# Attention outputs turned by DMA instead of TensorE transposes, the causal mask in one pass, and a new order in the group

## The reference

```python
xn = layernorm(x)                              # x: 8 x 1024 x 256, fp32
Q, K, V = xn @ wq.T, xn @ wk.T, xn @ wv.T      # 16 heads of 16 channels
Q, K = rope(Q), rope(K)
scores = where(causal, Q @ K.T / sqrt(16), -inf)
attn = softmax(scores) @ V                     # 8 x 1024 x 256
s = attn @ wo
g = silu(ffn(xn))                              # hidden 768, integer weights / 127
out = x + s * g
```

## Time and profile before

| | us |
|---|---|
| median of 3 runs | 1221.46 (1220.7 to 1222.96) |
| the profiled execution: its own time | 1220.83 |
| its span in the trace | 1219.1 |
| PE busy | 1176.2 (96%) |
| DVE busy | 971.1 (80%) |
| ACT busy | 880.6 (72%) |
| POOL busy | 638.2 (52%) |

### The profile page before, as it was taken

How to read it: one execution, slowest core, us unless ns; L and a number is a source line. 1 busy time by engine, 2 the same in 40 slices (tenths; PEclk the granted TensorE clock), 3 DMA queues, 4 the chain that set the end, 5 groups by cost and what they waited for, 6 DMA issues and landing times.

```text
span 1219.1 us, 29979 instructions
## 1 busy us (share of the span) xinstructions
PE 1176.2 (96%) x10707; PEld 554.8 (46%) x10707; DVE 971.1 (80%) x1160; ACT 880.6 (72%) x1123; POOL 638.2 (52%) x996
## 2 busy tenths in 40 slices
PE   5999999999999889999999999999999999999997
PEld 3565556656555333334444443444444444444333
DVE  6666666667777689988898899889888988898843
ACT  4554554454444588788888888888888888888884
POOL 5765665765564322444455445554565455445554
PEclk9999999999999899999999999999999999999998
DMA  9755454566642511332323313333144133332122
GB/s 254 191 173 155 141 187 135 157 191 172 167 136 87 147 45 46 98 79 72 97 76 110 97 46 106 73 103 97 49 122 113 45 98 88 97 97 58 59 71 88
DMA packets 157888, 134.81 MB, mean 111 GB/s; under 512 B 49472, under 2 KB 142144, under 8 KB 157760
## 3 DMA queue, kind: packets, MB, share of 16 engines
q1 hardware_dynamic: 157760, 133.08, 38.7%
HBM read 72.61 MB, written 50.33 MB: 101 GB/s over the span
## 4 chain that ended last, share of the span: by engine, by line
PE 61%; ACT 2%; DVE 1%; issue 1%; POOL 1%; ACTq 0%; DVEq 0%; POOLq 0%
PE ps L1380 23%; PE ps L1363 14%; PE ps L794 12%; PE ps L1410 4%; PE ps L802 3%; PE ps L1394 3%; PE ps L1402 2%; ACT pr L1281 1%; DVE mxp L818 1%; PE ps L833 1%; ACT on L1293 0%; POOL ah L1101 0%; POOL zt L1119 0%; DVE yt L1219 0%; ACT ot L1288 0%
## 5 line engine op out<-in xcount | busy, mean ns | idle before, releaser
L818 DVE TENSOR_REDUCE mxp<-ps 128x2 f32<-128x1024 f32 (+2 forms) x576 | 685.3, 1221 | 91.0 <-PE ps L802 50.6
L1281 ACT ACTIVATE pr<-ps 128x1024 f32<-128x1024 f32 x576 | 575.8, 1023 | 100.5 <-PE ps L1363 86.1
L1380 PE MATMUL ps<-pr,vt 128*32 128x512 f32 (+3 forms) x3072 | 315.3, 497 | 0.6 <-POOL pr L1091 0.5
L1363 PE MATMUL ps<-qs,ks 50*128 50x512 f16 (+3 forms) x1536 | 225.6, 329 | 8.6 <-DVE mxp L818 4.2
L794 PE MATMUL ps<-ks,qs 48*128 48x512 f16 (+2 forms) x1792 | 225.2, 304 | 8.2 <-ACT pr L1281 4.8
L1091 POOL TENSOR_SCALAR_AFFINE_SELECT pr<-pr 128x256 f32<-128x256 f32 (+1 forms) x448 | 191.6, 454 | 51.3 <-ACT pr L1281 51.0
L1363 PEld LDWEIGHTS ps<-qs,ks 50*128 50x128 f16 x1536 | 65.4, 93 | 212.7 <-issue 201.6
L674 PE MATMUL ps<-xTh,wguT 128*128 128x512 f16 x384 | 145.8, 380 | 1.2 <-ACT vs L558 1.1
L674 PE MATMUL ps<-xTl,wguT 128*128 128x512 f16 x384 | 145.5, 379 | 0.0
L794 PEld LDWEIGHTS ps<-ks,qs 48*128 48x128 f16 x1792 | 83.0, 94 | 98.6 <-issue 85.0
L849 POOL TENSOR_SCALAR mp<-mneg 32x128 f16<-32x128 f32 x32 | 9.3, 289 | 206.3 <-issue 200.9
(11 more groups left out here) (104 smaller groups left out, 1355.9 us busy)
## 6 DMA issues: line engine op xcount, KB each, us to landing
v_d<-vs SPq DMA_DIRECT2D x16, 1024.0 KB, 5.3
vt<-v_d SPq DMA_DIRECT2D x32, 512.0 KB, 4.0
xs<-in_L_attn_x SPq DMA_DIRECT2D x16, 512.0 KB, 4.5
q_parts_d<-parts SPq DMA_DIRECT2D x16, 512.0 KB, 3.0
k_parts_d<-parts SPq DMA_DIRECT2D x16, 512.0 KB, 3.1
gate_d<-gs SPq DMA_DIRECT2D x16, 512.0 KB, 3.2
qs<-q_parts_d SPq DMA_DIRECT2D x64, 128.0 KB, 3.1
ks<-k_parts_d SPq DMA_DIRECT2D x64, 128.0 KB, 3.1
```

The lines of the kernel that those rows point to most:

```text
L818: dve.tensor_reduce(dst, ps[:, slot:slot + 2, :].rearrange("p t (n s) -> p (t n) s", s=w), axis=AX.X, op=ALU.max).then_inc(keep["max_dve"] ...
L1281: act.activation(probs(step, s).rearrange("p (t j) s -> p t j s", t=2)[:, :, hs[0]:hs[-1] + 1, 0:w], ps[:, slot:slot + 2, 0:w * len(hs)].r ...
L1363: ins = pe.matmul(ps[:, slot + t, o:o + w], ks[g][r, j, kb * P:(kb + 1) * P], qs[g][r, j, lo:lo + w], start=o == 0, stop=True, skip_group_ ...
L1380: ins = pe.matmul(ps[VW * j:VW * (j + 1), O0, lo - c * CH:CH], vt[g % 2][:, kb, j, :], probs(step, s)[:, j, at:at + w], start=first, stop= ...
```

## The change

1. V is written with 16 columns of ones a head, so each sum comes on 16 rows. `take_output` stays; then SP moves each head's 16 rows of values into `oc` and its 16 rows of sums into `sc`, by DMA from `ot` (eight DMAs of 32 KB a half, `move_output`). In `oc` and `sc` the channels are on the partitions, 128 at a time, as the product with wo wants them. L1394, the copies `on`, `an` and `ah`, the transposes L1402 and the copies L1298 go.
2. Per tile: DVE takes the reciprocal of `sc` (128 x 256), POOL multiplies `oc` by it and splits the result into `aT`.
3. The mask: `pick` and `future` hold factors over 64 rows whose products give the mask of a 128 x 128 square, so one pass does. POOL builds them in two lots, in chunks (0, 1) and (5, 0).
4. `transpose_max` uses a transpose instead of a product with the identity.
5. ORDER, V_AT and all places in the group are new. In the last group DVE does the scaling and the additions of seven tiles; at the end the splits are shared by ACT, DVE and POOL.

```diff
-        ORDER = "EMEMEMEMEMEMEEMEMEMMEMEMEMEMEMEMEMEM"
+        ORDER = "EMEMEMEMEMEMEMMEMEMEMEMEMEMEMEMEMEEM"
...
-            V_AT = (9, 12, 16, 23, 27, 30, 35, TURNS + 1, TURNS + 4, TURNS + 6)
+            V_AT = (13, 16, 18, 24, 30, 33, 35, TURNS + 2, TURNS + 5, TURNS + 8)
-            TAKE1, OUT1, NORM1 = 3, 18, 14
-            TAKE0, OUT0, NORM0 = 8, 21, 14
-            MAXT, NEG, SPLIT_AT = 25, 12, 10
-            HALVE, ADD = (0, 7), (8, 17)
-            COPY, SCALE = (11, 9), (17, 12)
-            TR, EV, WO, MUL = (7, 26), (4, 13), (15, 33), (8, 16)
+            TAKE1, TAKE0, MAXT, NEG, SPLIT_AT = 5, 8, 25, 12, 11
+            INVERT, HALVE, ADD = (0, 3), (1, 6), (7, 13)
+            WO, MUL = (11, 21), (7, 10)
...
+                def move_output(step, c):
+                    b, g = step
+                    if g == 0 and b > 1:
+                        sp.wait_ge(t_lo.sem, t_lo.after((b - 2, (c + 1) * CT - 1)))
+                    sp.wait_ge(o_act.sem, o_act.after(step, c + 1))
+                    for j in range(GH):
+                        r, o = g % 2 * GH * DK + j * DK, j * VW
+                        sp.dma_start(oc[b % 2][r:r + DK, g // 2, c * CH:(c + 1) * CH], ot[o:o + DK, c]).then_inc(o_in[b % 2][c], 16)
+                        sp.dma_start(sc[b % 2][r:r + DK, g // 2, c * CH:(c + 1) * CH], ot[o + DK:o + VW, c]).then_inc(o_in[b % 2][c], 16)
...
+                def scale_tile(tile):
+                    pool.wait_ge(t_rec.sem, t_rec.after(tile))
+                    pool.tensor_tensor(columns(oc, tile), columns(oc, tile), columns(sc, tile), ALU.mult).then_inc(t_norm.sem, 1)
...
+                def invert_sums(tile):
+                    b, t = tile
+                    dve.wait_ge(*landed((b, NG - 1), t // CT))
+                    dve.reciprocal(columns(sc, tile), columns(sc, tile)).then_inc(t_rec.sem, 1)
...
                 def take_output(step, c):
-                    act.wait_ge(o_pe.sem, o_pe.after(earlier(step, 1), c + 1))
+                    if step != (0, 0):
+                        act.wait_ge(*landed(nth(step, -1), c))
...
-        for half in range(2):
-            for t in range(2):
-                r = slice(t * TILE, (t + 1) * TILE)
-                o = ps[:, slot + t, :].rearrange("p (n s) -> p n s", s=w)[:, :, w - P + half * TILE:w]
-                ins = pe.matmul(o, pick[r, half ^ t, :], future[r, half ^ t, 0:len(pieces), half * TILE:P],
-                                start=False, stop=half == 1, skip_group_check=True)
+        for t in range(2):
+            r = slice(t * TILE, (t + 1) * TILE)
+            o = ps[:, slot + t, :].rearrange("p (n s) -> p n s", s=w)[:, :, w - P:w]
+            ins = pe.matmul(o, pick[r, :], future[r, :].unsqueeze(1).to_broadcast([TILE, len(pieces), P]),
+                            start=False, stop=True, skip_group_check=True)
...
-    pe.matmul(ps[0:GH * QB, bank, at:at + P], keep["mxa"][step[1] % 2][:, :], keep["ident"][:, :],
-              start=True, stop=True).then_inc(keep["mx_t"].sem, 1)
+    pe.transpose(ps[0:GH * QB, bank, at:at + P], keep["mxa"][step[1] % 2][:, :], keep["ident"][:, :]).then_inc(keep["mx_t"].sem, 1)
...
+                    for run, first in RUNS:
+                        factor(pick, first, run, 0, run // 2, 1.0)
+                        factor(future, first, run, run // 2, run, MASKED)
+                    for d in range(LEAF - 1):
+                        factor(pick, 0, LEAF, d, d + 1, 2.0 ** (-LEAF_STEP * d))
+                        factor(future, 0, LEAF, d + 1, d + 2, -2.0 ** (LEAF_LEAST + LEAF_STEP * d))
```

More of the change, by code:

```diff
@@ L520, in chunk @@
                         constants()
+                    for t in range(2):
+                        if isinstance(step[0], int) and step == MASK_MADE[t]:
+                            mask_factors(t)
                 over_batches(pool, chunk)
@@ L890, in attention_phase @@
         ot = sb("ot", [P, 2, CH], F32)
[L891 to L894, removed]
+        oc = [sb(f"oc{i}", [P, KD, S], F32) for i in range(2)]
+        sc = [sb(f"sc{i}", [P, KD, S], F32) for i in range(2)]
         gt = sb("gt", [P, HALVES, CT, D], F32)
@@ L1053, in group @@
                     if prev:
+                        move_output(nth(step, -1), 1)
                         if ahead(step, 1):
@@ L1063, in group @@
                         load_output(b, 0)
+                    move_output(step, 0)
                     if ahead(step, 1):
@@ L1082, in _ @@
             def _(pool):
-                for s in (causal, t_hi, t_lo, t_mul, t_add):
+                for s in (causal, t_hi, t_lo, t_norm, t_mul, t_add):
                     s.start(pool)
@@ L1136, in group @@
                             mask(step, diag_units.index(u))
[L1137 to L1140 removed]
                         for i in range(2):
                             if u == HALVE[i] and tiles[i]:
+                                scale_tile(tiles[i])
                                 split_tile(tiles[i])
@@ L1163, in _ @@
+                for tile in end_tiles[0::2]:
+                    add_gated(tile).then_inc(s_end[0], 1)
             @block.vector
             def _(dve):
-                for s in (o_rec, o_norm):
-                    s.start(dve)
-                def invert_sums(step, c):
-                    dve.wait_ge(o_norm.sem, o_norm.after(earlier(step, 1), c + 1))
-                    dve.wait_ge(o_copy.sem, o_copy.after(step, c + 1))
-                    dve.reciprocal(rec[:, c], on[:, c].rearrange("p (r v) -> p r v", v=VW)[:, :, DK]).then_inc(o_rec.sem, 1)
@@ L1251, in last_group, with sums, result @@
-                    normalise(step, 1)
+                    def sums(i):
+                        invert_sums(last_tiles[i])
+                        scale_tile(last_tiles[i])
+                    def result(i):
+                        gate_product(last_tiles[i], tile_bank(i))
+                        dve.wait_ge(t_add.sem, t_add.after(earlier(last_tiles[i], 1)))
+                        add_gated(last_tiles[i]).then_inc(t_add.sem, 1)
+                    for i in range(3):
+                        sums(i)
@@ L1253, in _ @@
+                    for i in range(3):
+                        result(i)
+                    for i in range(3, len(last_tiles)):
+                        sums(i)
+                    for i in range(3, len(last_tiles)):
+                        result(i)
                 over_groups(group, last_group)
                 for tile in end_tiles:
-                    split_tile(tile)
+                    invert_sums(tile)
+                    scale_tile(tile)
                 for i, tile in enumerate(end_tiles):
-                    b, t = tile
+                    if i % 2 == 0:
+                        dve.wait_ge(t_lo.sem, t_lo.after(earlier(tile, 1)))
+                        low_part(tile)
@@ L1310, in group @@
                         for i in range(2):
-                            if u == EV[i] and tiles[i]:
-                                if i == 1:
-                                    act.wait_ge(mx_neg.sem, mx_neg.after(nth(step, 1)))
-                                take_tile(tiles[i], M0)
                             if u == MUL[i] and tiles[i]:
@@ L1469, in last_group @@
                             times_v(step, s)
-                    transpose_output(step, 1, freed=o_norm)
                 over_groups(group, last_group)
```

248 lines of the change are left out of this document (79 added, 169 removed).

## The result

The changed kernel is slower: **1302.72 us** (median of 4 runs, 1300.14 to 1303.27) against 1222.21 for the kernel before, run beside it; ratio 1.0659, 95% interval 1.0644 to 1.0674. The forecast of 1196 had the wrong sign and its range (up to 1252) was missed by 51 us.

A forecast was written before the change was run, and what follows sets the result against it. PE was taken as full in groups with tiles, DVE second and then longest. Groups with tiles -21.6, first batch -7, end +3: -25.6 us against 1220.83, forecast 1196, range 1174 to 1252.

The forecast's parts named there:

- I take 0.75: On DVE, two new reciprocals of 128x256 in each group with tiles: 0.75 us each, between bounds 0.41 and 1.54.
- dear reciprocal: Rival, chance 0.28: each group's two DVE reciprocals cost 0.79 us more each, +46 to 1242; kernel slower from 1.19 us each.
- I take 0.8: DVE's idle time in a group falls from 2.56 us to 0.8, bounds 0 and 2.56, giving 23.7 us with tiles.
- the banks keep the engines in step: Rival, chance 0.12: score banks leave DVE its 2.56 us idle per group, +55 to 1250, or 1230 with cheap reciprocals.
- cheap reciprocal: Rival, chance 0.20: DVE's reciprocal streams at 0.41 us, 0.34 less x 58, -20, giving 1176.
- -2.9 us: PE's work in a group with tiles falls by 2.9 us, from 24.45 to about 21.5.
- First batch: Its four groups, without reciprocals, each get 1.8 us shorter: -7 us.
- cost nothing: Sixteen more DMA issues a group on SP, 0.46 us apart, 7.4 us in all, delay nothing.
- SP becomes late: Rival, chance 0.08: in 14 groups loading for the gate, the next group starts 1.2 us late, +17, 1213.
- First phase: Two POOL mask lots of about 5 us each, largely in 3.73 us of idle time: net 0.
- The end: From last copy to first projection 7.4 us instead of 4.0, later tiles closer together: net +3, between -1 and +9.

The follow-up runs named there:

- kernel 9: The changed kernel with the mask's POOL steps in pairs, spread over the chunks, and the sums' DMAs issued by ACT behind single exponentials: 1283.27 us, ratio 1.051.
- kernel 10: As kernel 9, with a streaming pass of the same shape in place of every reciprocal of the sums: 1213.98 us, ratio 0.9943.
- Experiment 11: As kernel 10, with the string of turns made strictly alternating, E M eighteen times: 1284.1 us, ratio 1.0532.
- experiment 7: The kernel before with the mask in one pass, its POOL steps spread, and the transpose for the maxima, nothing else: 1215.58 us, ratio 0.9957.
- experiment 1: The changed kernel with each reciprocal of 128x256 replaced by a streaming tensor-scalar of the same shape: 1253.31 us, ratio 1.0256.
- experiment 3: The changed kernel with the old mask, two passes on PE, built in the first chunk: 1299.46 us, ratio 1.0637.
- experiment 6: The changed kernel with the mask's POOL steps in pairs, four or five at a time, between POOL's other work: 1295.91 us, ratio 1.0618.
- experiment 8: The kernel before with two further reciprocals of 128x256 on a scratch buffer in each group with tiles: 1294.21 us, ratio 1.0598.
- experiment 4: The changed kernel with the four DMAs of the sums of each move issued by ACT instead of SP, four at once: 1439.74 us, ratio 1.1767.

## Why the prediction was wrong

With these runs the difference can be put down to its parts. Unless said otherwise, spans of groups; the last of the 27 is a shorter one (24.09 in kernel 9, 21.90 in kernel 10, 22.63 before).

| part | us | from |
|---|---|---|
| reciprocals, in 27 groups | +59 | 26 x (26.34 - 24.15) + 24.09 - 21.90 |
| reciprocals, at the end | +7 | last group and end, 55.7 (kernel 9) less 48.6 (kernel 10) |
| new order without them | -9 | 26 x (24.15 - 24.47) + 21.90 - 22.63 |
| late moves and clock, in the groups | +9 | what is over the plain group: 9.8 after (6.0 of it waits for `qs<-mp`), 1.2 before |
| the rest of the end | +8 | 14.9 less 7.1 |
| first phase, and four groups | +6 | 6.7 and -1.0 |

They sum to 80, the 79.3 us of span but for rounding.

**The reciprocal, the step that failed first.** "I take 0.75" is the sentence. The trace had 182, 231 and 245 ns for sixteen elements, and I took the fastest as the true rate and called the slower one a start-up. It is the other way round: 0.143 + 16 x 6.25 ns = 0.243 us is the slow one, and the 182 ns is the second of a pair, which begins while the first still runs. The pair's joint length, 0.35 us, is one fixed part and twice 0.100 us, so the rate stood in the trace; I used that length only for overlap. The mechanism of the rival "dear reciprocal" was right, its deciding point (1.19 us) was passed by far, and even its price of 1.54 us was too low; it had 0.28. An operation known only at 16 elements was extrapolated to 256, sixteen times, and the forecast then stood on the cheap side of its own bounds. The estimate from the eight steps of the Trainium skill, "VectorE: DVE Perf Modes", section "First, the fixed hardware budget", 2.25 us, lies 0.51 above the measured 1.74, my upper bound 0.20 below it. The measured 6.25 ns an element are six times the 1.03 of a streaming pass, not eight: the page's rule pointed the right way, and I argued it away with the 182 ns. The prices went by 58 reciprocals, where the trace has 64: 53 in the 27 groups' own places, 7 of the last group's tiles and 4 at the end.

**DVE's idle time**, "I take 0.8", failed too: 1.55 us was left in the plain group after, 24.79 busy of 26.34. With 22.9 + 2 x 1.0 for the true reciprocal and 1.5 of idle time, the sum's own form gives the measured group: 26.4. The rival "the banks keep the engines in step" was right as well: 24.15 us in kernel 10, where PE had 1.25 and DVE 1.6 us spare. So even the "cheap reciprocal" (1176) could not have come true: kernel 10 takes 1214. Experiment 11 bears the rival out: the order of the turns alone moves a group by 2.0 us at the same busy time of PE.

**PE**, "-2.9 us": busy time fell from 24.45 to 23.10, -1.35. The mask and the maxima's transpose bring 0.36 (experiment 7), where I counted 0.75; the transposes' places gave PE about 1.0, not 2.1. I had counted whole distances from start to start; that this is the reason wasn't tested. It didn't matter, as PE no longer bound.

**First batch**, -7: measured -1.0. Same cause as above: its groups went from 24.45 to 24.1, whatever DVE and PE had to spare, and the last of the four ends 0.9 us late, waiting for `qs<-mp`.

**SP**, "cost nothing": a move's issue is 0.63 us and not 0.46, and the next group's first product came late, as the rival "SP becomes late" said; it gave +17 for 14 groups, and the waits are 6.0 us in the 27 groups beside the slow reciprocals and 20 in experiment 1 without them. The mechanism was right in its place: loads and stores stand between the two moves and push the second, with the maxima behind it.

**The clock** had no term. It fell in five groups with tiles; where it alone made a group longer that is 0.2 to 1.9 us, 2.4 in all.

**First phase**, net 0: +6.7. Steps cost 0.5 and not 0.3 us, the lots come to 8 us each and not 5, and I took the 3.7 us of idle time for cover of both. By experiments 3, 6 and 8, whose first groups start at 413.8 to 414.0, the lots cost some 8.5; the trace of before starts its own 1.7 us later than experiment 8, with the same first phase.

**The end**, +3 (to +9): +14.9 with the last group. I charged one reciprocal before the first projection; DVE does all four first, at 1.74 us. And a second wait of the same kind stands within the last group: DVE waits 7.48 us at 1260.01 for the moves of the half before.

What stays open: why the place of ten M turns is worth 2 us, which string would bring a group under 24.1, and why the clock falls in some groups and not in others with the same waits. The parts of the end other than the reciprocals weren't separated.

## What to carry to other kernels

An operation whose price the trace has only at a small size is to be priced at the slowest record of a sequence, with the fixed part taken off; if the whole forecast hangs on it, the dearer price deserves the larger chance, and a run like experiment 8, the operation at its new size in the old kernel, settles it. Before moving work from a full engine to one with some idle time, look whether the idle time is one piece: in this ring of three slots a block of 1.7 us was felt at nearly full price. And an operation that costs six streaming passes an element belongs ahead of a replication: the sums repeated on sixteen rows made sixteen times as many elements to invert.

## What the runs showed of the hardware

- DVE's reciprocal in fp32: 6.25 ns an element and partition, with 0.143 us fixed (943 ns at 128 columns, 1743 at 256), where a streaming pass over 256 takes 0.46 us in the median (experiment 1).
- The issue of a DMA between on-chip buffers (16 rows of 2 KB) holds SP 0.63 us, that of the loads 0.46; on ACT one takes 0.52, four at once 2.44 us, in which the engine was idle for 1.60; over the run that took 147 us more than one at a time.
- POOL's select over 128x32 (single elements, every fourth) takes 0.41 us, over 128x64 from 0.24 us (0.24 to 0.26 in most, up to 0.66).
- PE's granted clock can fall amid groups that are all alike: 0.88 over one of the changed kernel and one of kernel 9, behind waits of 0.79 and 0.51 us, and both took 28.20 us in place of 26.34; 0.79 over one in experiment 4. Waits alone don't decide it: kernel 8, with 1.02 and 1.55 us, stayed at 1.00.
